# First attention: GpSimd masks the weights and ScalarE sums them, statistics are taken early; in roped attention the gathers, the first block and the PSUM banks are rearranged

## The chip, the cores and the metric

The kernel runs on one core of one Trainium2 chip, in one launch. Its time is the device time in microseconds, the median of several runs. PE is TensorE, DVE VectorE, ACT ScalarE, POOL GpSimd, SP the sync engine that issues most DMAs.

## The reference

Four layers, each of an attention and a feed-forward part, act on x (4 batches of 256 tokens, width 256) with a context of 1601 rows a batch; every part reads the layer-normed x and adds its result to x. The parts that matter here:

```
L0 attention:  Q = z @ Wq.T;  scores = coef * Q @ K_mem.T          # K_mem = V_mem = context, one head
               thr = 54th largest score of the row
               scores = where(scores < thr, -inf, scores)
               att = softmax(scores);  x += (att @ V_mem) @ W_o.T
L0 ffn:        top-2 of 8 experts; each token's two expert outputs, times its shares, are added to x
L1 attention:  16 query heads, 4 key heads of 128; q, k rms-normed, weighted, rotated (rope by position);
               keys = context + the 256 tokens (1857);  softmax(q @ k.T / sqrt(128)) @ v @ Wo.T
L3 attention:  the same without rope and with the context's keys alone (1601)
```

Everything is fp32. Products that need more than the PE's single pass are done as hi*hi + hi*lo + lo*hi, with hi and lo halves in fp32r.

## The kernel before

**First attention** (`memory_attention`). The 1024 queries are eight tiles j = 0..7 of 128, two a batch: b = j // 2, q = j % 2. Each engine runs its own queue, in an order written out in the code, and waits on semaphores.

PE per batch: `items(b)` (the context is turned to keys in eight pieces CX, the normed tokens NX, two projections Q; each is also split in hi and lo), `scores(b, q)`, `turn_weights(b, q)` (transposes the masked weights), `weighted(b, q)` (weights times context rows), `project(b, q)`. Its order is: turn_weights(b-1, 1), items(b+1) with weighted(b-1, 1) between its pieces, scores(b+1, 0), project(b-1, 1), turn_weights(b, 0), weighted(b, 0), scores(b+1, 1), project(b, 0). ACT keeps the raw scores (`keep`), takes exp, copies the turned weights (`take_weights`), and takes the high half of each item and output; a piece of an item goes back and forth between PE and ACT.

DVE finds the threshold. For each j it sorts the 1601 scores into four sets (`sort`, six two-input operations), then takes 28 steps of MAX8 and MATCH_REPLACE8 (`select`). Beside the sort and the first steps of j runs `merge(j - 1)`, eleven small operations of which the last gives the threshold of tile j-1. Right behind it, at step 5, came `mask(j - 1)`: one scalar_tensor_tensor (is_ge, then times exp) which also sums the row, and a reciprocal. At fixed steps DVE takes `output_low` and `add_output` of tile j-2: steps 2 and 7 in an even j, 14 and 20 in an odd one (OUTPUTS). At step 7 of an even j stood `row_stats(b + 1)`, at step 13 `normalise(b + 1)`. turn_weights of tile j waits for mask_ok; its second piece waits for y_done of tile j-1.

**Roped attention** (`grouped_attention` with rope). A first block (FIRST_TASKS) prepares batch 0 and head 0; then 16 groups (batch, key head) of 30 turns run, each group with two units of 15 key tiles (KT = 15). In turn n every engine does its part of score tile n, then the tasks of that turn in the list GROUP_TURNS; values(n) follow 21 turns later, the shift 18 turns later (on POOL for t % 4 == 0 and t >= 13, else on DVE), exp 20 turns later. Tasks work for the next group: KV (project one key tile), KN/KR (norm and rotate four key tiles; on POOL, in the first block on DVE), Q/QN/QR (queries; POOL), KX/QX (transposes), RA (nine steps on DVE that make angles of positions) and RS (their sines on ACT), W (split weights in hi and lo), OX/Y (output), MX/NB (row maxima), PX/PR (positions). `name<` is the task for the group before.

GP(j) on POOL gathers one of 16 expert outputs into a ring of four buffers (pairs j, two for each of 8 token tiles), GA(j) on DVE adds it to x; GP(j) waits for GA(j-4). Four pairs are in the first block, twelve in group 0.

PSUM: score tile n goes to bank SCORE_BANKS[n % 3] = (0, 1, 4); `scores(n)` on PE waits until `highest(n - 3)` on DVE has read its bank (`peaked`), or `keep(n - 3)` on ACT for the first tile of a unit. Items take ITEM_BANKS in turn, two in the groups: item i waits for `item_free` of item i-2. The second grouped attention (a3, no rope, KT = 13, 26 turns) has the same code and its own lists.

Of the kernel before, what the change touches and what calls it, by code (L numbers as in the profile page):

```python
# [151 lines left out]
def memory_attention(nc, m, w):  # L152
# [17 lines left out]
    with Stage(nc, "a0") as st:  # L170
        zt = [st.sb(f"zt{i}", [P, DC, S], F32R) for i in range(2)]
        ct = [st.sb(f"ct{i}", [P, DC, CTXP], F32R) for i in range(2)]
        stats, mv, rstd, z = (st.sb("stats", [P, QT, 6]), st.sb("mv", [P, QT, 2]), st.sb("rstd", [P, 2, QT]),
# [11 lines left out]
        best = st.sb("best", [P, 8])  # L185
# [10 lines left out]
            st.sem(n) for n in "item_ready item_hi item_rest item_free s_ready raw_ok neg_ok exp_ok mask_ok".split()]  # L196
        taken, padded, sort_ok, merged, minus_ok, pt_turned, pt_ok, o_ready, o_hi, o_lo, y_ready, y_done = [
# [50 lines left out]
        with nc.Block(name="a0_all") as block:  # L248
# [194 lines left out]
            def _(act):  # L443
# [67 lines left out]
                for b in range(B):  # L511
                    if b:
                        take_weights(b - 1, 1)
                        exp(b, 0)
# [9 lines left out]
                    take_weights(b, 0)  # L524
                    take_output(b, 0)
                    if b + 1 < B:
                        keep(b + 1, 1)
                take_weights(B - 1, 1)
                take_output(B - 1, 1)

            @block.gpsimd
            def _(pool):
# [4 lines left out]
                for b in range(B):  # L537
                    pool.wait_ge(var_ok, b + 1)
                    pool.tensor_tensor(rstd[:, 1, :], rstd[:, 0, :], m.nhalf[:, 0:1].to_broadcast([P, QT]),
                                       ALU.pow).then_inc(rstd_ok, 1)  # L540
# [3 lines left out]
            def _(dve):  # L544
                step = Step(dve, dstep)

                def row_stats(b):
                    for q in range(QT):
                        ins = dve.bn_stats(stats[:, q, :], m.x[:, QT * b + q, :])
                    step(ins)  # L550
                    for q in range(QT):
                        ins = dve.bn_aggr(mv[:, q, :], stats[:, q, :])
                    step(ins)
                    dve.tensor_scalar(rstd[:, 0, :], mv[:, :, 1], 1e-5, None, ALU.add).then_inc(var_ok, 1)

# [54 lines left out]
                def merge(j):  # L610
# [3249 lines left out]
```

## Time and profile before

| | us |
|---|---|
| median of 3 runs (lowest, highest) | 3559.38 (3558.9, 3567.83) |
| the profiled execution | 3562.59 |
| its span | 3560.9 |
| mean granted clock of PE in it | 0.959 |

| engine | busy us | share of the span |
|---|---|---|
| PE | 3303.9 | 93% |
| DVE | 2288.8 | 64% |
| ACT | 2254.4 | 63% |
| POOL | 1548.8 | 43% |

A busy share is an average over stages with different limits. A row of a timeline reads: start, duration of the merged instructions, engine, line, operation, out<-in, shapes, count; and in brackets the idle time of the engine before it and what ended it. Neighbouring instructions on DVE and ACT overlap by some 0.1 us at their ends, so the step from one start to the next is a little shorter than the duration.

### The profile page before, as it was taken

The page shows a single profiled execution, that of the slowest core. Times are in us where ns is not written, and L with a number is a line of the kernel's source. Part 1 is how long each engine was busy: PE and PEld are TensorE (multiplying, and loading weights), DVE is VectorE, ACT ScalarE, POOL GpSimd, SP SyncE. Part 2 cuts the span into 40 slices and gives each one's busy share as a digit, 9 for nine tenths or more (in the row PEclk, how much of TensorE's full clock was granted, in tenths as well). Part 3 has the DMA queues.
Part 4 walks back from the last instruction along what each step waited for, and adds up shares of the span by engine and source line. Part 5 has one row for each costly group of instructions (what it writes and reads, how often), then busy time and mean ns, then how long its engine had stood idle before and what let it go on. Part 6 is the DMA issues. An engine that isn't in the chain of part 4 may idle for free. (4 is left out here: it accounts for less than half of the span.)

```text
span 3560.9 us, 64151 instructions
## 1 busy us (share of the span) xinstructions
PE 3303.9 (93%) x23332; PEld 2863.1 (80%) x23332; DVE 2288.8 (64%) x4549; ACT 2254.4 (63%) x5204; POOL 1548.8 (43%) x1568
## 2 busy tenths in 40 slices
PE   6858968999999999998899999898999999999989
PEld 5658956889989989997666666587999999999888
DVE  8976756776676676666777777535655555555544
ACT  3426746777777777775476676516777777777743
POOL 0012136776676667673120220103555555555534
PEclk8879978999999999999899999899999999999999
DMA  5206522211120120001201000113221121110011
GB/s 191 93 25 230 213 101 69 87 61 37 43 79 31 37 91 31 31 19 50 86 1 38 10 29 1 77 38 119 77 77 60 42 73 42 64 64 31 31 39 39
DMA packets 74457, 227.83 MB, mean 64 GB/s; under 512 B 7780, under 2 KB 29472, under 8 KB 69152
## 3 DMA queue, kind: packets, MB, share of 16 engines
q1 hardware_dynamic: 67538, 184.04, 14.6%
q0 software_dynamic: 3696, 37.68, 2.8%
q8 instruction: 188, 3.08, 0.4%
q10 hardware_dynamic: 2910, 2.01, 0.2%
q14 instruction: 125, 1.02, 0.1%
HBM read 178.60 MB, written 45.11 MB: 63 GB/s over the span
## 5 line engine op out<-in xcount | busy, mean ns | idle before, releaser
L1188 PE MATMUL ps<-a_v_rows,a_ring 128*128 128x129 f32 (+1 forms) x7168 | 934.9, 275 | 15.2 <-DVE a_o_rows L1598 14.6
L1572 DVE SCALAR_TENSOR_TENSOR a_peak<-ps,a_k_rstd,a_peak 128x512 f32<-128x512 f32 (+1 forms) x768 | 575.8, 750 | 557.7 <-ACT a_ring L1309 546.5
L1309 ACT ACTIVATE a_ring<-ps,a_k_rstd 128x512 f32<-128x512 f32 (+1 forms) x896 | 618.2, 691 | 479.1 <-PE ps L1178 439.7
L1188 PEld LDWEIGHTS ps<-a_v_rows,a_ring 128*128 128x128 f32 (+1 forms) x7168 | 874.7, 191 | 35.5 <-issue 18.6
L1436 POOL TENSOR_TENSOR a_ring<-a_ring,a_negb 128x512 f32<-128x512 f32 (+1 forms) x506 | 645.6, 1297 | 266.0 <-ACT a_negb L1318 258.5
L1324 ACT ACTIVATE a_ring<-a_ring 128x512 f32<-128x512 f32 (+1 forms) x896 | 564.6, 633 | 12.3 <-DVE a_ring L1589 11.5
L1176 PE MATMUL ps<-a_qt,a_kt 128*128 128x512 f32 (+1 forms) x896 | 424.5, 474 | 9.4 <-DVE a_peak L1572 4.4
L1076 PEld LDWEIGHTS ps<-a_wr,a_ct 128*128 128x128 f32 (+1 forms) x2496 | 352.4, 189 | 57.4 <-issue 14.1
L1076 PE MATMUL ps<-a_wr,a_ct 128*128 128x256 f32 (+1 forms) x2496 | 374.0, 287 | 20.5 <-DMA a_ct<-ctx_lo 13.9
L1178 PE MATMUL ps<-a_qt,a_kt 128*128 128x512 f32 (+1 forms) x896 | 356.0, 397 | 0.0
L1177 PE MATMUL ps<-a_qt,a_kt 128*128 128x512 f32 (+1 forms) x896 | 354.6, 396 | 0.0
L3431 ACT ACTIVATE a_probs<-ps 128x1024 f32<-128x1024 f32 x224 | 229.9, 1026 | 135.4 <-PE ps L3285 134.7
L1589 DVE TENSOR_TENSOR a_ring<-a_ring,ps 128x512 f32<-128x512 f32 x390 | 263.0, 677 | 2.8 <-ACT a_negb L1318 2.8
L3623 DVE TENSOR_REDUCE a_parts<-ps 128x1 f32<-128x448 f32 x384 | 222.2, 619 | 57.3 <-PE ps L3247 52.2
L1178 PEld LDWEIGHTS ps<-a_qt,a_kt 128*128 128x128 f32 (+1 forms) x896 | 166.3, 186 | 42.7
L1176 PEld LDWEIGHTS ps<-a_qt,a_kt 128*128 128x128 f32 (+1 forms) x896 | 169.7, 189 | 13.0 <-issue 6.3
L1177 PEld LDWEIGHTS ps<-a_qt,a_kt 128*128 128x128 f32 (+1 forms) x896 | 169.7, 189 | 1.7
L3285 PE MATMUL ps<-a_qt,a_kt 128*128 128x512 f32 x448 | 164.3, 448 | 2.5 <-ACT a_qt L3418 2.3
L1371 POOL TENSOR_SCALAR a_k_sq<-a_k_sq 128x4 f32<-128x4 f32 (+2 forms) x128 | 29.9, 233 | 310.6 <-ACT a_v_rows L1272 306.1
L1520 DVE TENSOR_TENSOR a_k_rows<-ps,a_kw 128x128 f32<-128x128 f32 (+1 forms) x448 | 126.6, 283 | 54.0 <-ACT a_v_rows L1272 53.8
L3247 PE MATMUL ps<-a_kt,a_qt 128*128 128x448 f32 (+1 forms) x512 | 154.7, 369 | 4.6 <-ACT a_kt L3399 1.1
L1268 ACT ACTIVATE a_square<-ps 128x128 f32<-128x128 f32 (+1 forms) x448 | 125.0, 279 | 36.9 <-PE ps L1076 30.6
(469 smaller groups left out, 6028.8 us busy)
## 6 DMA issues: line engine op xcount, KB each, us to landing
a_wr<-a_w SPq DMA_DIRECT2D x96, 512.0 KB, 4.4
a_w<-a_wr SPq DMA_DIRECT2D x32, 512.0 KB, 3.9
a_wr<-a_w SPq DMA_DIRECT2D x48, 256.0 KB, 3.6
a_ct<-ctx_hi SPq DMA_DIRECT2D x8, 1090.0 KB, 6.1
a_ct<-ctx_lo SPq DMA_DIRECT2D x8, 1090.0 KB, 8.8
f_we<-in_f_experts SPq DMA_DIRECT2D x8, 1088.0 KB, 8.3
ctx_hi<-a_ct SPq DMA_DIRECT2D x4, 1602.0 KB, 5.4
ctx_lo<-a_ct SPq DMA_DIRECT2D x4, 1602.0 KB, 9.3
```

What stands on the lines that cost most here:

```text
L1076: ins = pe.matmul(out[0:r, 0:2 * HD], src, wr[0][v][:, c * 2 * HD:(c + 1) * 2 * HD], start=(n == 0), stop=(n == 3 * DC - 1))
L1176: pe.matmul(out, kt[0][:, at:at + r], qt[0][:, cols], start=True, stop=False)
L1177: pe.matmul(out, kt[0][:, at:at + r], qt[1][:, cols], start=False, stop=False)
L1178: pe.matmul(out, kt[1][:, at:at + r], qt[0][:, cols], start=False, stop=True).then_inc(st_ready, 1)
L1188: ins = pe.matmul(m.ps[:, 6 + i // 2, (i % 2) * 256:(i % 2) * 256 + VW], slot(n)[0:r, i * P:(i + 1) * P], v_rows[u // NG % 2][0:r, t, :], ...
L1309: act.activation(slot(n)[0:r, :], m.ps[0:r, SCORE_BANKS[n % 3], :], ACT.Copy, scale=k_rstd[0:r, g % 2, t:t + 1]).then_inc(kept, 1)
L1324: act.activation(slot(n)[0:r, :], slot(n)[0:r, :], ACT.Exp).then_inc(exp_done, 1)
L1436: pool.tensor_tensor(slot(n)[0:r, :], slot(n)[0:r, :], negb[0:r, u % 2, :], ALU.add)\
L1572: dve.scalar_tensor_tensor(out=peak[0:r, :], in0=m.ps[0:r, SCORE_BANKS[n % 3], :], scalar=k_rstd[0:r, u // NG % 2, t:t + 1], in1=(slot(n - ...
L1589: dve.tensor_tensor(slot(n)[0:r, :], slot(n)[0:r, :], m.ps[0:r, MAX_BANK, :], ALU.add)\
L3431: act.activation(flat2(probs[n % 3][:, :, :]), flat2(m.ps[:, first:first + 2, :]), ACT.Exp)\
L3623: dve.tensor_reduce(to, slot(("R", h, j))[:, 0:n], AX.X, ALU.max, negate=True).then_inc(neg_done, 1)
```

## The change

In first attention, `mask` goes to POOL as two passes (is_ge against the threshold into a new tile `above`, then times exp in place), ACT sums the masked row in a copy with an accumulator (`sum_weights`, behind each `take_weights`), and DVE takes the reciprocal at `add_output`. The threshold is handed on by a nop on DVE behind a wait for the last MAX8, and `best` gets two buffers. The statistics of batches 1 to 3 are taken at once ahead of the first sort, in `powers(1)` on POOL too, and `normalise(b + 1)` moves from step 13 to step 7.

```
+                def sum_weights(b, q):                                  # ACT
+                    act.wait_ge(mask_ok, j + 1)
+                    act.activation(raw[b % 2][:, q, 0:CTX], expd[:, q, :], ACT.Copy, accum_out=rsum[:, 0, q:q + 1])\
+                       .then_inc(sum_ok, 1)
...
                     if b:
                         take_weights(b - 1, 1)
+                        sum_weights(b - 1, 1)
                         exp(b, 0)
                     if b + 1 < B:
                         items(b + 1)
...
                     take_weights(b, 0)
+                    sum_weights(b, 0)
                     take_output(b, 0)
...
                 take_weights(B - 1, 1)
+                sum_weights(B - 1, 1)
                 take_output(B - 1, 1)
...
+                def mask(b, q):                                         # POOL
+                    j = QT * b + q
+                    pool.wait_ge(chosen, j + 1)
+                    pool.tensor_scalar(above[:, :], raw[b % 2][:, q, 0:CTX], best[j % 2][:, AT:AT + 1], None, ALU.is_ge)\
+                        .then_inc(above_ok, 1)
+                    pool.wait_ge(above_ok, j + 1)
+                    pool.wait_ge(exp_ok, j + 1)
+                    pool.tensor_tensor(expd[:, q, :], expd[:, q, :], above[:, :], ALU.mult).then_inc(mask_ok, 1)
...
-                        dve.max(out=best[:, :], in_=rest).then_inc(merged, 1)
+                        if r == 0 and j >= 2:
+                            dve.wait_ge(above_ok, j - 1)
+                        ins = dve.max(out=best[j % 2][:, :], in_=rest).then_inc(merged, 1)
+                        if r == LEFT_ROUNDS - 1:
+                            dve.wait_ge(merged, base + 2 * LEFT_ROUNDS - 1)
+                            dve.engine_nop().then_inc(chosen, 1)
...
                 def add_output(b, q):
+                    dve.wait_ge(sum_ok, QT * b + q + 1)
+                    step(dve.reciprocal(rsum[:, 1, q:q + 1], rsum[:, 0, q:q + 1]))
                     dve.wait_ge(y_ready, QT * b + q + 1)
...
                 dve.wait_ge(xs_in, 16)
+                row_stats(range(QT, TT))
...
-                        if j and i == FOLLOW:
-                            mask(*divmod(j - 1, QT))
...
                         if q == 0 and b + 1 < B and i == FOLLOW + 2:
-                            row_stats(b + 1)
-                        if q == 0 and b + 1 < B and i == FOLLOW + 8:
                             normalise(b + 1)
```

In roped attention the two lists of turns change, and in both grouped attentions the banks:

```
 GROUP_TURNS True:
-        "Y0< KR6< PR0 GP4 GP5", "MX1 KR7< GP6 GP7", "NB1 KX2< W0< PX0", "Q0 RA0 GA4 GA5 GP8 GP9", "Y1< RS0",
-        "Q1 GA6 GA7 GP10 GP11", "KX3<", "QN0 W2< RA1 RA2 GA8 GA9 GP12 GP13", "KV0 QN1", "KV1 QR0 GA10 GA11 GP14 GP15",
-        "KV2 QR1", "KV3 QR2 RA3 GA12 GA13", "OX0 KN0 QR3 GA14 GA15", "KV4 KR0", "KV5 KR1", "KV6 W1 RA4", "MX0", "NB0 QX0",
-        "KV7 RA5", "KX0 KN1", "KV8 KR2", "KV9 KR3", "KV10 RA6", "OX1 N0", "KV11", "KX1 KN2", "KV12 KR4 RA7",
-        "KV13 KR5 NZ0", "KV14 RA8", "QX1 KN3 NX0",
+        "Y0< KR6< PR0 GP4 GP5 GP6 GP7", "MX1 KR7<", "NB1 KX2< W0< PX0", "Q0 RA0 GA12< GA13<", "Y1< RS0 GA14< GA15<", "KX3<",
+        "Q1", "W2<", "KV0 QN0 GA4 GA5", "KV1 QN1 GA6 GA7", "KV2 QR0", "KV3 QR1 RA1 RA2", "OX0 KN0 QR2", "KV4 QR3", "KV5 KR0",
+        "KV6 W1 KR1 RA3 GP8", "MX0 GP9", "NB0 QX0 GP10", "KV7 RA4 GP11", "KX0 KN1", "KV8 KR2", "KV9 KR3", "KV10 RA5 RA6 GA8",
+        "OX1 N0 GA9", "KV11 GA10", "KX1 KN2 GA11", "KV12 KR4 RA7 GP12", "KV13 KR5 NZ0 GP13", "KV14 RA8 GP14",
+        "QX1 KN3 NX0 GP15",
 FIRST_TASKS True:
-        "GP0 V0 GP1 GP2 GP3 PR0 PX0 GA0 GA1 RA0 RA1 GA2 GA3 RA2 N0 RA3 KV0 NZ0 KV1 RA4 NX0 KV2 V1 KV3 RA5 Q0 KV4 RA6 "
-        "Q1 KV5 QN0 RA7 KV6 QN1 RA8 KV7 RS0 KN0 KR0 KV8 KR1 KN1 KX0 KV9 QR0 KR2 KV10 QR1 KR3 KV11 KX1 QR2 KN2 QR3 W1 "
-        "KV12 KR4 QX0 KV13 KR5 KV14 KX2 KN3 QX1 KR6 W0 KR7 KX3"
+        "GP0 V0 GP1 GP2 GP3 PR0 PX0 RA0 RA1 RA2 GA0 GA1 GA2 GA3 N0 RA3 KV0 RA4 NZ0 KV1 V1 RA5 NX0 KV2 RA6 KV3 RA7 Q0 KV4 Q1 "
+        "RA8 RS0 QN0 KV5 KR0 KN0 QN1 KV6 KR1 KX0 KV7 QR0 KN1 KR2 KV8 QR1 KR3 KV9 KX1 KV10 QR2 KV11 KN2 QR3 KR4 KV12 KR5 "
+        "QX0 W1 KV13 KX2 KV14 KN3 KR6 QX1 KR7 W0 KX3"
...
-    SCORE_BANKS, MAX_BANK = (0, 1, 4), 5
+    SCORE_BANKS, MAX_BANK = (0, 1), 5
-            ITEM_BANKS = (2, 3) if attend else (2, 3, 6, 7)
+            ITEM_BANKS = (2, 3, 4) if attend else (2, 3, 6, 7)
...
-                        if n >= 3:
-                            if (n - 3) % KT:
-                                pe.wait_ge(peaked, peaks(n - 3))
-                            else:
-                                pe.wait_ge(kept, n - 2)
+                        if n >= 2:
+                            if (n - 2) % KT:
+                                pe.wait_ge(peaked, peaks(n - 2))
+                            else:
+                                pe.wait_ge(kept, n - 1)
```

The other uses of the score bank (in `scores`, `keep` and `highest`) go from `n % 3` to `n % 2`.

## Rows read from the trace of the kernel before

**Rows 1.** The windows by stage: busy us of each engine, granted clock, DMA share, GB/s.
```profile
0.00:240.00 240.00, 171.37 (x961) 145.86 (x961) 210.96 (x604) 81.20 (x142) 5.46 (x18) 0.82 0.29 106
...
480.00:540.00 60.00, 27.81 (x130) 24.70 (x130) 35.16 (x66) 19.97 (x75) 25.53 (x31) 0.61 0.33 119
...
540.00:605.00 65.00, 53.41 (x289) 44.35 (x290) 43.19 (x70) 40.25 (x109) 47.44 (x49) 0.84 0.24 78
...
605.00:1665.00 1060.00, 1040.42 (x7550) 955.90 (x7549) 720.17 (x1248) 781.90 (x1937) 705.20 (x713) 1.00 0.14 49
```

**Rows 2.** DVE's timeline in first attention: start us, us, instruction, idle before.
```profile
25.46 1.90 DVE L585 TENSOR_TENSOR a_sorting<-a_raw 128x802 f32<-128x802 f32 x2 [4.49 <-ACT a_raw L474]
...
34.53 0.73 DVE L549 BATCH_NORM_STATS2 a_stats<-x_slots 128x6 f32<-128x256 f32 x2
...
167.09 0.47 DVE L643 SCALAR_TENSOR_TENSOR x_slots<-ps,a_rsum,x_slots 128x256 f32<-128x256 f32 x1
...
180.84 0.28 DVE L618 MAX8 a_best<-a_found 128x8 f32<-128x120 f32 x1
...
181.50 1.88 DVE L629 SCALAR_TENSOR_TENSOR a_expd<-a_raw,a_best,a_expd 128x1601 f32<-128x1601 f32 x1
```

**Rows 3.** PE's timeline in first attention.
```profile
39.59 1.08 PE L301 MATMUL ps<-ident,a_z 128*128 128x128 f32 x4 [3.60 <-DVE a_z L561]
...
133.78 0.65 PE L373 MATMUL ps<-ident,a_expd 128*128 128x128 f32 x4 [0.74 <-DVE a_rsum L632]
...
164.31 0.94 PE L413 MATMUL ps<-a_wr,a_ot 128*128 128x256 f32 x6 [0.27 <-DVE a_ot L636]
...
183.82 0.60 PE L373 MATMUL ps<-ident,a_expd 128*128 128x128 f32 x4
...
227.21 1.97 PE L373 MATMUL ps<-ident,a_expd 128*128 128x128 f32 x8 [5.81 <-DVE a_rsum L632]
```

**Rows 4.** POOL's groups by form: busy us, mean ns, idle before.
```profile
L3478 POOL TENSOR_TENSOR a_k_rows<-a_k_rows,a_norm_w 128x1024 f32<-128x1024 f32 x6 | 14.3, 2391 | 0.5
...
L3477 POOL TENSOR_TENSOR a_k_rows<-a_k_rows,a_sq 128x1024 f32<-128x1024 f32 x6 | 11.4, 1898 | 0.5
...
L1798 POOL CAST f_wr<-f_wf 128x1024 fp32r<-128x1024 f32 x14 | 14.5, 1038 | 92.0 <-PE ps L1905 92.0
```

**Rows 5.** Line L1436 by itself: duration ns min/median/max, first and last start.
```profile
L1436 POOL TENSOR_TENSOR a_ring<-a_ring,a_negb x506: 1257/1285/2317, 579.4 to 3418.1; 128x512 f32<-128x512 f32 x128, 65x512 f32<-65x512 f32 x41
```

**Rows 6.** ACT's timeline in first attention.
```profile
137.06 1.62 ACT L481 ACTIVATE a_expd<-a_raw,a_negm 128x1601 f32<-128x1601 f32 x1
```

**Rows 7.** ACT's, DVE's and PE's timelines in roped attention's first block.
```profile
510.02 1.28 ACT L1331 ACT_TABLE_LOAD   x1
...
510.69 0.65 DVE L1645 TENSOR_SCALAR a_ang_tmp<-a_ang_tmp 128x960 f32<-128x960 f32 x1
...
515.73 1.08 PE L1105 MATMUL ps<-ident,a_k_rows 128*128 128x128 f32 x4 [5.52 <-DVEq L1534]
...
537.70 0.77 PE L1105 MATMUL ps<-ident,a_k_rows 65*128 65x65 f32 x3 [3.92 <-DVEq L1534]
```

**Rows 8.** DVE's, PE's and POOL's timelines in group 0 of roped attention.
```profile
561.48 3.79 DVE L1498 SCALAR_TENSOR_TENSOR x_slots<-a_z,share,x_slots 128x256 f32<-128x256 f32 x2 [2.28 <-DMA a_z<-y_slots,slot]
...
565.99 0.80 PE L1176 MATMUL ps<-a_qt,a_kt 128*128 128x512 f32 x1 [4.39 <-DVE a_peak L1572]
...
578.52 0.73 POOL L1399 TENSOR_TENSOR a_k_rows<-a_by_cos,a_by_sin 128x256 f32<-128x256 f32 x1
```

**Rows 9.** PE's waits in roped attention: us in total, times, longest.
```profile
PE ps L1133 <- DVE a_qt L1489: 3.5, 3, 1.2
```

**Rows 10.** PE's timeline in a steady group of roped attention.
```profile
836.36 2.02 PE L1188 MATMUL ps<-a_v_rows,a_ring 128*128 128x129 f32 x16 [0.30 <-DVE a_o_rows L1598]
```

**Rows 11.** PE's and DVE's timelines, second grouped attention, turns 20 and 18.
```profile
2475.77 0.40 PE L1176 MATMUL ps<-a_qt,a_kt 128*128 128x512 f32 x1
...
2476.95 0.75 DVE L1572 SCALAR_TENSOR_TENSOR a_peak<-ps,a_k_rstd,a_peak 128x512 f32<-128x512 f32 x1 [2.17 <-ACT a_ring L1309]
```

More of the change, by code:

```diff
@@ L184, in memory_attention @@
         found = [st.sb(f"found{i}", [P, FOUND, 8]) for i in range(2)]
-        best = st.sb("best", [P, 8])
+        best = [st.sb(f"best{i}", [P, 8]) for i in range(2)]
+        above = st.sb("above", [P, CTX])
         expd = st.sb("expd", [P, QT, CTX])
@@ L196, in memory_attention @@
             st.sem(n) for n in "item_ready item_hi item_rest item_free s_ready raw_ok neg_ok exp_ok mask_ok".split()]
+        chosen, above_ok, sum_ok = [st.sem(n) for n in "chosen above_ok sum_ok".split()]
         taken, padded, sort_ok, merged, minus_ok, pt_turned, pt_ok, o_ready, o_hi, o_lo, y_ready, y_done = [
@@ L536, in _, with powers @@
                     pool.memset(ct[i][:, :, CTX:CTXP].bitcast(F32), 0.0).then_inc(zeroed, 1)
[L537 to L540, printed above, removed]
+                def powers(part, cols):
+                    pool.wait_ge(var_ok, part + 1)
+                    pool.tensor_tensor(rstd[:, 1, cols], rstd[:, 0, cols],
+                                       m.nhalf[:, 0:1].to_broadcast([P, cols.stop - cols.start]), ALU.pow).then_inc(rstd_ok, 1)
+                def mask(b, q):
+                    j = QT * b + q
+                    pool.wait_ge(chosen, j + 1)
[4 more added lines that the diff above has]
+                    pool.tensor_tensor(expd[:, q, :], expd[:, q, :], above[:, :], ALU.mult).then_inc(mask_ok, 1)
+                powers(0, slice(0, QT))
+                powers(1, slice(QT, TT))
+                for j in range(QT * B):
+                    mask(*divmod(j, QT))
                 token_powers(pool, m, "f0", EARLY)
@@ L621, in merge @@
                             dve.wait_ge(merged, base + 2 * r + 1)
-                            dve.match_replace(out=rest, in_to_replace=best[:, :], in_values=rest, imm_value=-3.0e38)\
+                            dve.match_replace(out=rest, in_to_replace=best[j % 2][:, :], in_values=rest, imm_value=-3.0e38)\
                                .then_inc(merged, 1)
                             yield
-                    dve.wait_ge(merged, base + 2 * LEFT_ROUNDS - 1)
-                def mask(b, q):
-                    dve.wait_ge(exp_ok, QT * b + q + 1)
-                    step(dve.scalar_tensor_tensor(out=expd[:, q, :], in0=raw[b % 2][:, q, 0:CTX],
-                                                  scalar=best[:, AT:AT + 1], in1=expd[:, q, :],
-                                                  op0=ALU.is_ge, op1=ALU.mult, accum_out=rsum[:, 0, q:q + 1]))
-                    dve.reciprocal(rsum[:, 1, q:q + 1], rsum[:, 0, q:q + 1]).then_inc(mask_ok, 1)
                 def output_low(b, q):
@@ L658, in _ @@
                 dve.wait_ge(x_in, 16)
-                row_stats(0)
+                row_stats(range(QT))
                 dve.wait_ge(kact, 2)
@@ L702, in _ @@
                 add_output(B - 1, 0)
-                mask(B - 1, 1)
                 dve.wait_ge(y_done, QT * (B - 1))
```

26 lines of the change are left out of this document (14 added, 12 removed).

## The prediction, made before the change was run

> **What bounds the kernel now.** I read the page first: PE is busy 93% of the span, so the question in each stage is what still makes PE wait. The windows give the stages [rows 1]: first attention 0 to 240 us (PE 171 of 240, DVE 211), roped attention's first block 480 to 540 (PE 28 of 60, granted clock 0.61), its group 0 from 540 to 605 (PE 53 of 65), its groups 1 to 15 (PE 1040 of 1060, clock 1.00). The two short stretches around 540 and the first attention have room; the long one has 20 us at most.
>
> In first attention j = 0..7 counts query tiles. DVE is gapless from 25.46 on in all but small pieces [rows 2], so it looks like the bound. But two of its steps wait for others. `add_output` of tile j-2 stands at step 20 of an odd j and needs PE's projection: for j = 5, PE ends it at 165.25 (164.31 + 0.94 [rows 3]), DVE takes it at 167.09 [rows 2], a slack of 1.84 us (1.44 for j = 3). And PE's `turn_weights` for tile 5 starts at 183.82 [rows 3] directly behind the mask (181.50 to 183.5 [rows 2]). So PE, ACT and DVE form a loop that is nearly closed: mask, turn, copies, exp, key items, scores, projection, `add_output`, end of j, merge, mask. That loop, and not the sum of DVE's work, is what I price.
>
> **First attention: the terms.** (1) The mask leaves DVE: 1.88 + 0.08, about 2.0 us a tile. (2) Statistics of b = 1 to 3, 0.73 + 0.25 + 0.17 from 34.53 on, about 1.13 us each, go into the 4.49 us in which DVE waited for the first raw scores [rows 2]: free. (3) `normalise` six steps earlier brings items(1) forward about 2.9 us (PE waited 3.60 us for z there, 39.59 [rows 3]). (4) A nop and a wait for the last MAX8, about 0.1 us; the threshold is handed on after that MAX8 (180.84 + 0.28 [rows 2]) and not at 181.50: 0.3 us earlier. (5) GpSimd's mask: no row shows it. The multiply is 1601 elements with two inputs; 1024 took 2.39 us [rows 4], hence 3.75 us (3.0 by the fastest two-input row, 1024 in 1.90 with a broadcast operand). The comparison has one input and a scalar: between the CAST row (1024 in 1.04, so 1.65 us) and the two-input row (3.75). I take 1.65, nearest in kind, and 0.2 for three handovers: 5.6 us, bounds 4.8 and 8. (6) ScalarE's sum: a 1601-element ACTIVATE takes 1.62 us [rows 6] and an accumulator read adds 0.1: 1.6 us a tile. For odd tiles it stands in ACT's queue ahead of exp(b+1, 0) and all key items of the next batch, for which PE waits (ACT is gapless there), so it counts in full. For even tiles PE's 8 us of weighted sums hide it, for tile 7 just so. (7) The reciprocal moves to `add_output`, ahead of its wait: hidden.
>
> Now the loop, tile 3's turn (133.78 [rows 3]) to tile 5's: before 50.0 us. After: + (5.6 - 2.0) for the mask, + 1.6 for the sum, - 1.84 of slack used up, - 0.3: +3.1 us. DVE has more than 5 us to spare at step 20, so its savings end in that wait. Step by step: tile 1's mask is ready at 84.2 (before 84.46: the earlier start just pays for GpSimd); tile 3's turn at 136.9 (+3.2); tile 5's at 189.5 (+5.7). In the last batch no items follow, DVE's saving counts again, tile 6's turn comes at 213.0 (+5.3), and since `output_low` of tile 6 holds the last merge, tile 7's at 235.8 against 227.21 [rows 3]: **+8.5 us** at the stage's end. The mask stands four times on this path: 4.8 us a mask gives +5, 8 us gives +18. What hides term (1) today is nothing; what makes it worthless is the wait at step 20.
>
> GpSimd's rate speaks against moving it. The Trainium skill (GPSIMD Engine Reference, section 3.1 Elementwise — side-by-side cycle accounting) puts a two-input operation at some 2.6 cycles an element and a one-input one near 1.03, at 1.2 GHz; an estimate from that page is 3.5 + 1.4 us, and the stage would then come out near +6. The rows above are slightly slower and stand.
>
> **First block of roped attention.** PE waits 5.52 us at 515.73 for the rotated keys, behind the sine tables (510.02 on ACT), behind the angles (510.69 + 0.65 on DVE) [rows 7]. The first three angle steps (2.5 us) now run in the gap before the gathered rows land, and the last one no longer stands behind two more projections' waits: I get angles at 508.1, tables at 510.0, first key transpose 2.8 us earlier. At the end the last rotation stands ahead of the weight split and not behind KX2, QX1 and W0: the last key transpose (537.70 [rows 7]) 2.4 us earlier. Rounded up for the smaller waits between: **-5.5 us** (bounds: 0, and -9 if half of PE's idle time goes).
>
> **Group 0.** GA8 to GA11 hold DVE for their gathers (2.28 us at 561.48 [rows 8]) and with it the scores: PE waits 4.39 at 565.99 [rows 8], and 3.50 and 1.09 in the 12 us after it. Twelve gathers, about 1.28 us each on POOL with issue, also stand among QN, QR and KR: keys 0 to 3 are rotated only at 579.25 (578.52 + 0.73 [rows 8]). In the new order only four stand ahead of them, before Q is there. POOL then has QN (4.3), four half rotations of q twice (8.2), KN0 (1.3), KR (4.0) from about 551 on: 569. PE's turn 19 needs it; four gathers (5.1) then delay the first shift to 574.4 and the turn of the first values from 585.7 to 576.6. **-9 us** (bounds -3, where POOL's later gathers delay the shifts, and -13, all of PE's waits and the slow clock).
>
> **Banks and steady groups.** The third item bank removes waits for item_free: 1.15 us three times (`Y`), 0.34 three times (`NX`), 1.48 once; the row of `Y`'s line sums 3.5 [rows 9]. `Q1` and `KX3` swapped: `outputs` now comes before Q1 on DVE, and the 0.30 us that PE waits for it in each of 12 groups (836.36 [rows 10]) goes; the three of 2.49 with the sine tables on ACT lose 0.2. Together 3.6 + 0.6 + 3.5 + 1.0 + 1.7 = 10.4. POOL's work shifted by a turn is hidden: QR3 is ready 7 us ahead of its reader. Against it, two score banks: scores(n) waits for peaked(n-2). I set each scores start against the end of the peak of two turns before: in groups past 0 the median margin is 1.2 to 3.5 us, so nothing is lost but about 0.3 us in the three groups with angle work. Roped groups: **-9.5 us** (bounds -2 and -11). In the second grouped attention the margins past group 0 are 0.64 us and up; in its group 0 they are negative: scores at 2475.77 started 1.93 us before that peak ended (2476.95 + 0.75 [rows 11]), turn 6 is short by 1.33. Less 0.8 for an item wait and recovery: **+2.5 us** (0 to +6).
>
> **Sum.** 8.5 - 5.5 - 9 - 9.5 + 2.5 = -13.0 us on the profiled execution's 3562.59 (3560.9 span and 1.7 around it). The median of the runs is 3.2 us below that execution, so I put it on the median: 3559.4 - 13.0 = 3546.4 us.
>
> **Rivals.**
> A. The group 0 and steady gains are small because POOL and the score banks take the waits' place: block -4, group 0 -3, steady -5, banks +3, first attention +8.5: 3559. For it: margins at turns 6, 7, 20 and 22 are the thinnest. Against it: POOL has idle time left in the second half of group 0 and half of the span [rows 1]. Chance 0.24.
> B. First attention gets faster: if ACT's sum and GpSimd's mask found slack that I don't see, DVE's 8 times 2 and 3.4 us would count, about -17 instead of +8.5: 3521. Against it: 1.84 us at step 20. Chance 0.09.
> C. Slower: GpSimd's mask is stretched by DVE, which is never idle in that stage. Rows show GpSimd's two-input operation from 1.26 to 2.32 us, median 1.29 [rows 5]. If both passes went at two-input rate and 1.75 times stretched, the mask would take 13.5 us, four times 7.9 more than I count: +40 in first attention, 3578. It decides from a mask of 11.5 us on (+32). Chance 0.09. The Trainium skill (SBUF — State Buffer, section Who interferes with whom) says that a DVE instruction with one SBUF input outside the two-port modes doesn't contend with GpSimd; MAX8 and MATCH_REPLACE8, which run behind the threshold, have one. No row here shows the pair.
> D. The change does what I say, within 8 us either way: 3546. Chance 0.58.
>
> **Chances.** D has 0.58, mostly beyond 0.3% (10.7 us, about what a measurement can tell from no change): 0.41 faster, 0.17 within. A is within: 0.22, 0.02 slower. B is faster, C slower. Faster 0.50, same 0.39, slower 0.11. The range 3533 to 3564 leaves out B, C and little else.
>
> **What would show it.** DVE waits for PE (y) at step 20 of j = 3 and 5, 5 us or more each; mask passes of 1.65 and 3.75 us on POOL; first attention ends near 249, not 240; group 0 starts 5.5 us sooner after its block's start and lasts 55; groups 4 to 6 take 69.25 and not 69.55; group 0 of the second one takes 44.5. If first attention ends before 238, or a steady roped group takes over 69.6, the prediction is wrong in its reasons.

## The result

The changed kernel takes 3568.27 us (median of 11 runs, 3565.64 to 3574.23), the kernel before 3563.39 us (11 runs, 3558.9 to 3567.83). The ratio is 1.0018, 95% interval 1.001 to 1.0027: slower by some 5 us. The forecast was 3546.4, with a range of 3533 to 3564: the result lies 22 us above the forecast and 4 above the range. Four of the 22 are no error of the forecast's terms: it stood on 3559.4, the median of the first three runs of the kernel before, and eleven runs give 3563.4. The profiled execution has a span of 3566.0 us, 5.1 more than before, where the forecast's terms summed to 13.0 less: 18 us apart.

The same stage boundaries in both profiled executions show where the forecast failed (the sum is taken before rounding). A boundary is the start of a PE instruction (the first transposes of the expert layer's z, the transpose of the positions, the first score tile of a group):

| stage | before, us | after, us | forecast | measured |
|---|---|---|---|---|
| first attention | 242.11 | 258.40 | +8.5 | +16.3 |
| first expert layer | 244.21 | 243.39 | 0 | -0.8 |
| roped attention, first block | 53.84 | 51.34 | -5.5 | -2.5 |
| its group 0 | 64.63 | 61.01 | -9 | -3.6 |
| its groups 1 to 14 | 987.74 | 978.61 | -9.5 | -9.1 |
| its last group, next layers | 854.14 | 855.34 | 0 | +1.2 |
| second grouped attention, group 0 | 42.04 | 45.89 | +2.5 | +3.9 |
| all behind it | 1072.2 | 1072.1 | 0 | -0.1 |
| sum | | | -13.0 | +5.2 |

### The profile page after: what moved, and what is told of

The parts are those of the page before. It is cut to its first block and busy times, and to the rows that moved or that the text cites. A ratio compares the mean times of both kernels' runs of the same rounds, so it can differ in the third digit from the quotient of the medians.

```text
span 3566.0 us, 64198 instructions
## 1 busy us (share of the span) xinstructions
PE 3298.7 (93%) x23332; PEld 2861.2 (80%) x23332; DVE 2279.9 (64%) x4531; ACT 2260.7 (63%) x5220; POOL 1606.0 (45%) x1582
## 5 line engine op out<-in xcount | busy, mean ns | idle before, releaser
L1393 POOL TENSOR_SCALAR a_k_sq<-a_k_sq 128x4 f32<-128x4 f32 (+2 forms) x128 | 28.8, 225 | 312.8 <-ACT a_v_rows L1294 308.3
```

## The profile after

The windows of the kernel after, for the stages of [rows 1] (columns as there: PE, PEld, DVE, ACT, POOL, granted clock, DMA share, GB/s):

```profile
0.00:258.40 258.40, 171.25 (x962) 145.51 (x962) 209.76 (x593) 93.54 (x158) 69.46 (x43) 0.81 0.27 98
501.80:553.00 51.20, 27.38 (x130) 25.04 (x130) 33.51 (x64) 19.48 (x74) 21.27 (x22) 0.63 0.31 114
553.00:614.00 61.00, 52.07 (x286) 43.71 (x287) 38.22 (x66) 39.64 (x108) 44.15 (x46) 0.90 0.24 79
614.00:1592.70 978.70, 970.25 (x7036) 894.43 (x7035) 671.04 (x1173) 732.08 (x1857) 676.77 (x693) 1.00 0.15 51
```

In first attention PE's busy time is that of before, 171 us, in a longer stage: the 16 us are waiting, not work. A stage's length in one execution isn't exact: over the profiles below, kernels with the same code in a stage differ by some 4 us in first attention, 3.7 in the first block (49.1 to 52.8 for the changed order, mean 50.6, with granted clocks of 0.63 to 0.74), and by 8.5 in the stage of the last group and the next layers (854.3 to 862.8). Group 0 of the second grouped attention repeats within 1 us, its other groups within 0.4.

POOL's two passes of the mask, by source line (ns min/median/max, first and last start):

```profile
L556 POOL TENSOR_SCALAR a_above<-a_raw,a_best x8: 4328/4330/4347, 55.6 to 236.4; 128x1601 f32<-128x1601 f32 x8
L560 POOL TENSOR_TENSOR a_expd<-a_expd,a_above x8: 3553/3564/3623, 60.0 to 240.8; 128x1601 f32<-128x1601 f32 x8
```

This is the row to read first. I had put the comparison at 1.65 us and the multiply at 3.75. The multiply came at 3.56, the comparison at 4.33, above the 3.75 of my two-input bound for it. The mask is ready 8.1 us behind the threshold: 5.6 were forecast, with 8 as the upper bound. All eight comparisons lie within 0.02 us, whatever DVE ran beside them, and the last multiply, at 240.83 when DVE was idle (from 240.78 to 253.99), took 3.55, the others 3.55 to 3.62: DVE doesn't stretch them.

PE's timeline at the turns of tiles 5, 6 and 7, against [rows 3]:

```profile
195.43 3.13 PE L375 MATMUL ps<-ident,a_expd 128*128 128x128 f32 x13 [7.91 <-POOL a_expd L560]
...
219.26 3.13 PE L375 MATMUL ps<-ident,a_expd 128*128 128x128 f32 x13 [10.08 <-POOL a_expd L560]
...
244.44 1.97 PE L375 MATMUL ps<-ident,a_expd 128*128 128x128 f32 x8 [11.39 <-POOL a_expd L560]
```

DVE's timeline at step 20 of j = 3 and 5 (`add_output` of tiles 1 and 3), against [rows 2], where DVE came to it without a wait:

```profile
118.52 0.48 DVE L669 SCALAR_TENSOR_TENSOR x_slots<-ps,a_rsum,x_slots 128x256 f32<-128x256 f32 x1 [4.50 <-PE ps L415]
...
173.19 0.48 DVE L669 SCALAR_TENSOR_TENSOR x_slots<-ps,a_rsum,x_slots 128x256 f32<-128x256 f32 x1 [3.86 <-PE ps L415]
```

So the loop is closed as forecast: what DVE saved by giving the mask away it spends here, and PE spends the mask's longer time at each turn.

PE's waits in roped attention's steady groups (after, 614 to 1665), against [rows 9]. The rows for `Y` and `NX` are gone, and two score banks cost 3.9. The wait for `outputs` fell to 5.3 from the 13.1 of the first row, which is the kernel before's (its groups 1 to 15, 605 to 1665):

```profile
PE ps L1188 <- DVE a_o_rows L1598: 13.1, 17, 2.5
PE ps L1210 <- DVE a_o_rows L1620: 5.3, 6, 1.1
PE ps L1198 <- DVE a_peak L1594: 3.9, 4, 1.1
```

## Experiments

The times stand beside the kernel before on the same chip in the same job (medians 3561.1 to 3562.3). Stages are read as in the table above. The changed first attention, in seven kernels that have it unedited, ended at 258.4 to 262.6, mean 260.7 (the profile after is the earliest of them); the one of before at 242.1 and 242.0 in two.

**The two halves.** Two kernels, each with a part of the diff undone: `memory_attention` (all that stands ahead of GROUP_TURNS) as changed and the rest as before; and the reverse.

> The kernel before with the whole edit of first attention and nothing of the roped one. My theory: the loop through add_output carries GpSimd's mask (8.1 us from the threshold on) four times, first attention's first expert transposes come at 258 us and not at 242, and nothing later gives it back: 15.5 us slower than the kernel before, 3579. Rival, the parts interact (the later entry into the expert stage changes PE's clock or a DMA): the two halves don't add up, this one is under 10 slower.

Measured: 3582.56 us, ratio 1.0051 (1.0037 to 1.0064): 18 us slower by the ratio, 21 by the medians. First attention ends at 262.61; no later stage differs from before by more than 3.8 us.

> The kernel before with the edit of the roped attention and of the banks alone, first attention as before. My theory: block -2.5, group 0 -3.6, steady groups -9.1, second attention's group 0 +3.9, rest 0: 11 us faster than before, 3552. Rival, interaction: more than 15 or less than 7 faster.

Measured: 3550.99 us, ratio 0.9967 (0.9955 to 0.9979), 12 us faster by the ratio, 11 by the medians, with block, group 0, steady groups and the second attention's group 0 at -3.0, -3.2, -9.1 and +4.0 (and +4.3 in the last group with the next layers, the stage that scatters most). The halves add up within the intervals: the change is a gain of 12 with a loss of 18 in front of it.

**The mask's price and its factor of four.** This kernel leaves the comparison out; the weights are multiplied by ones.

```
-                    pool.tensor_scalar(above[:, :], raw[b % 2][:, q, 0:CTX], best[j % 2][:, AT:AT + 1], None, ALU.is_ge)\
-                        .then_inc(above_ok, 1)
+                    if j == 0:
+                        pool.memset(above[:, :], 1.0).then_inc(above_ok, 1)
+                    else:
+                        pool.engine_nop().then_inc(above_ok, 1)
```

> The changed kernel with GpSimd's compare left out (the weights are multiplied by ones; the rest of first attention as it is): the mask is 3.6 and not 8.0 us behind the threshold. Loop theory: 4.35 us taken off a path that passes the mask four times, less what the waits at add_output (4.50 and 3.86 us) can give: 13 to 17 us faster than the changed kernel, expert transposes near 244. Rival 1, the loss comes from VectorE being held up while GpSimd's passes run (1.6 + 3.3 + 1.8 + 3.3 us seen at the two normalise pairs): only the part under the compare goes, about 5 us faster. Rival 2, ScalarE's sum carries the loss: under 3 us faster.

Measured: 3550.89 us, 17.4 below the changed kernel's 3568.27 (ratio to before 0.9967, 0.9955 to 0.9979; 16 us when each is set against the kernel before of its own job), and first attention ends at 241.27 and not at 258.40: 17.1 us for a pass of 4.33, so about four times (19.4 against the mean of the seven). By turns the gain is uneven: 1.7 us up to tile 1's turn, then 5.1, 3.5 and 7.8 up to those of tiles 3, 5 and 7. Rivals 1 and 2 are out. PE's timeline of this kernel at tile 3's turn (in the changed kernel it started at 140.75, after 7.90 us of waiting):

```profile
133.92 1.32 PE L375 MATMUL ps<-ident,a_expd 128*128 128x128 f32 x5 [3.55 <-POOL a_expd L562]
```

**Which of the comparison's properties makes it slow.** `best[j % 2][:, AT:AT + 1]` replaced by the number 0.0.

> The changed kernel with GpSimd's compare against the number 0 in the place of the tile's threshold (another set of weights is kept). The compare took 4.33 us, 2.7 ns an element, against my 1.65. Theory 1, that is what GpSimd takes for an is_ge on 1601 fp32 elements of a row: again 4.3 us, and the time of the changed kernel. Theory 2, the scalar held in SBUF, one for each partition, makes it slow: 1.6 to 3 us, and four times the difference comes off first attention (5 to 11 us).

Measured: 3569.1 us, ratio 1.002 (1.0011 to 1.0029). Its row by source line:

```profile
L556 POOL TENSOR_SCALAR a_above<-a_raw x8: 4257/4260/4282, 56.2 to 237.3; 128x1601 f32<-128x1601 f32 x8
```

Theory 1: GpSimd took 2.7 ns an element for this is_ge on fp32, more than for its two-input multiply (2.2). The operand from SBUF adds 0.07 us. Whether another operation in the same one-input form is faster, no run shows; the CAST of [rows 4] (1.0 ns) is another instruction.

**ScalarE's sum.** In ACT's order `sum_weights(b - 1, 1)` goes behind `items(b + 1)` (and `exp` waits for the sum of two tiles before).

> The changed kernel with ScalarE's sum of the odd tiles behind the next batch's key items instead of ahead of exp and those items. Loop theory: 1.6 us comes off the path at tiles 1, 3 and 5, the sum of tile 7 stays: 4 to 5 us faster than the changed kernel. Rival, the sum is hidden in GpSimd's mask time or delays the raw scores now: within 1 us.

Measured: 3567.4 us, ratio 1.0014 (1.0005 to 1.0023), 0.9 below the changed kernel; first attention ends at 256.90, 1.5 below the profile after and 3.8 below the mean of the seven. The forecast 4 to 5 us didn't come: the intervals of the two kernels overlap, and set against the kernel before of its own job this one is no faster than the changed one. So the sum costs less than the 1.6 us a tile that I counted in full. In the profile after PE waited only 0.90 us behind tile 3's sum, beside its own weighted sums:

```profile
148.03 0.50 PE L327 MATMUL ps<-a_ct,a_minus_r 128*128 128x512 f32 x1 [0.90 <-ACT a_ct L452]
```

How much of 0 to 4 us the three sums really cost, the runs don't tell.

**Normalise beside GpSimd's mask.**

```
-                        if q == 0 and b + 1 < B and i == FOLLOW + 2:
+                        if q == 0 and b + 1 < B and i == FOLLOW + 8:
```

> The changed kernel with normalise back at step 13, when GpSimd's mask of the tile before is over. In the changed kernel its two instructions took 1.99 + 3.72 and 2.50 + 3.72 us against 0.40 alone. Loop theory: VectorE gets some 5 us back twice, and they end in the wait at add_output (4.50 and 3.86 us): within 2 us of the changed kernel, the waits there grow. Rival, VectorE is held up by GpSimd and that is the loss: 5 to 10 us faster.

Measured: 3568.44 us, ratio 1.0018 (1.0009 to 1.0027): no change of the time, and DVE's waits at add_output grew from 4.50 and 3.86 to 5.7 and 5.0. In its profile first attention ended at 263.5, 0.9 above the longest of the seven, and not earlier. VectorE is held up, but off the path.

**Group 0: the gathers.** In the changed profile the first shift on POOL (590.10) stands behind three gathers. ACT's exp waits for it; behind that exp in ACT's queue stands the next `keep`, DVE's peak waits for that `keep`, and with two banks PE's score waits for that peak. POOL's, ACT's, DVE's and PE's timelines there:

```profile
586.50 1.08 POOL L1466 DMA_INDIRECT a_z<-y_slots,slot  x1 [0.31 <-POOL a_k_rows L1421]
587.89 0.95 POOL L1466 DMA_INDIRECT a_z<-y_slots,slot  x1 [0.30 <-issue]
589.14 0.95 POOL L1466 DMA_INDIRECT a_o_rows<-y_slots,slot  x1 [0.30 <-issue]
590.10 1.28 POOL L1458 TENSOR_TENSOR a_ring<-a_ring,a_negb 128x512 f32<-128x512 f32 x1
...
591.42 0.63 ACT L1346 ACTIVATE a_ring<-a_ring 128x512 f32<-128x512 f32 x1 [2.45 <-POOL a_ring L1458]
591.96 0.67 ACT L1331 ACTIVATE a_ring<-ps,a_k_rstd 128x512 f32<-128x512 f32 x1
...
592.66 0.75 DVE L1594 SCALAR_TENSOR_TENSOR a_peak<-ps,a_k_rstd,a_peak 128x512 f32<-128x512 f32 x1 [3.76 <-ACT a_ring L1331]
...
593.46 0.80 PE L1198 MATMUL ps<-a_qt,a_kt 128*128 128x512 f32 x1 [3.60 <-DVE a_peak L1594]
```

```
-        "KV6 W1 KR1 RA3 GP8", "MX0 GP9", "NB0 QX0 GP10", "KV7 RA4 GP11", "KX0 KN1", "KV8 KR2", "KV9 KR3", "KV10 RA5 RA6 GA8",
-        "OX1 N0 GA9", "KV11 GA10", "KX1 KN2 GA11", "KV12 KR4 RA7 GP12", "KV13 KR5 NZ0 GP13", "KV14 RA8 GP14",
-        "QX1 KN3 NX0 GP15",
+        "KV6 W1 KR1 RA3", "MX0", "NB0 QX0", "KV7 RA4 GP8", "KX0 KN1 GP9", "KV8 KR2 GP10", "KV9 KR3 GP11", "KV10 RA5 RA6",
+        "OX1 N0", "KV11 GA8", "KX1 KN2 GA9 GP12", "KV12 KR4 RA7 GA10 GP13", "KV13 KR5 NZ0 GA11 GP14", "KV14 RA8 GP15",
+        "QX1 KN3 NX0",
```

> The changed kernel with GP8 to GP11 of group 0 three turns later (turns 18 to 21, behind that turn's shift), and GA8 to GA11 and GP12 to GP15 after them. My theory: the first shift waited 2.45 us behind ScalarE's row and GpSimd's three gathers (586.5 to 590.1), and with it exp, keep(20), its bank and the scores (3.6 us): group 0 takes 57.5 and not 61.0, 3.5 us faster. Rival 1, the shift waits for KR1, which ends 33 us after the group's start: under 1 us. Rival 2, the gathers now stand among the later shifts and take it back: 0 or slower.

Measured: 3565.94 us, ratio 1.0014 (1.0005 to 1.0023), group 0 at 61.70. Turns 21 and 22 (from one score tile's start to the next) fell from 5.18 and 5.91 us to 2.74 and 3.22, and turns 25, 27 and 28 rose from 2.0, 2.3 and 2.3 to 3.34, 4.92 and 3.62: rival 2.

Only the fall of turn 21 is the wait of my theory. In turn 22 of the changed kernel PE never waits after its scores have begun; it runs at the lower clock (granted 0.51, near the 1.2 GHz level, against 1.00, 2.4 GHz, in this kernel's turn 22), behind a turn in which it was busy for 1.6 of 5.2 us. The windows of turns 21 and 22 of the changed kernel (columns as above):

```profile
588.28:593.46 5.18, 1.58 (x11) 1.24 (x9) 1.42 (x4) 2.73 (x8) 4.55 (x6) 0.90 0.32 89
593.46:599.38 5.92, 5.92 (x26) 5.63 (x26) 4.21 (x8) 3.37 (x11) 5.67 (x6) 0.51 0.03 11
```

Turn 28 of this kernel, with a clock of 0.62 behind the long turn 27, repeats it. Turn 27 shows something new. The addition GA9 on DVE took 3.63 us and not 0.48, until POOL's chain of three passes was through, and the peak and the scores stood behind it (this kernel's timelines of POOL, DVE, PE):

```profile
606.51 1.30 POOL L1458 TENSOR_TENSOR a_ring<-a_ring,a_negb 128x512 f32<-128x512 f32 x1
607.75 1.28 POOL L1413 TENSOR_TENSOR a_by_sin<-a_k_rows,a_cs 128x512 f32<-128x512 f32 x1
608.98 1.26 POOL L1414 TENSOR_TENSOR a_by_cos<-a_k_rows,a_cs 128x512 f32<-128x512 f32 x1
...
606.91 3.63 DVE L1520 SCALAR_TENSOR_TENSOR x_slots<-a_z,share,x_slots 128x256 f32<-128x256 f32 x1
610.46 0.74 DVE L1594 SCALAR_TENSOR_TENSOR a_peak<-ps,a_k_rstd,a_peak 128x512 f32<-128x512 f32 x1
...
611.26 0.50 PE L1198 MATMUL ps<-a_qt,a_kt 128*128 128x512 f32 x1 [2.38 <-DVE a_peak L1594]
```

The next kernel leaves gathers and additions of pairs 8 to 15 out (`return g == 0 and i < 8`).

> The changed kernel with only pairs 4 to 7 gathered and added in group 0; pairs 8 to 15 are left out (eight expert outputs are not added to x). Theory 1: the eight gathers and additions are what keeps group 0 from the forecast 55.6 us: group 0 takes 56. Theory 2: the chain of queries and keys on GpSimd, which ends 33 us after the group's start, keeps it: 59 or more.

Measured: group 0 takes 56.02 us (the whole 3560.18, ratio 0.9996, 0.9987 to 1.0005). Theory 1: the eight gathers with their additions are worth 5.0 us there, nearly the whole distance to the forecast 55.6. Two turns hold it: turn 21 fell by 2.4 us (the wait) and turn 22 by 2.7 (the clock, 1.00 here). The chain of queries and keys still ended 33 us after the group's start. The group behind it, whose first turns lose four additions too, took 67.0 and not 68.6.

**The first block.** In FIRST_TASKS:

```
-        "QX0 W1 KV13 KX2 KV14 KN3 KR6 QX1 KR7 W0 KX3"
+        "W1 KV13 KX2 KV14 KN3 QX0 KR6 QX1 KR7 W0 KX3"
```

> The changed kernel with the first block's end in another order: QX0 stands behind KV13, KX2, KV14 and KN3 and not ahead of them. My theory: the block's keys became early as forecast, and its end is now set by GpSimd's query chain, for which PE waited 4.06 us with two projections and a key transpose queued behind: the block takes 4 us less, 47 and not 51. Rival, the last keys' chain (projection, norm on GpSimd, rotation on VectorE, transpose) is as long: under 1 us.

Measured: 3562.31 us, ratio 1.0001 (0.9992 to 1.001), 6 us below the changed kernel. The block takes 46.77 us and not 51.34 (47.3 and 48.1 in the two later kernels with this order; the mean of eleven with the changed order is 50.6, so some 3 us are its worth). PE's timeline of the changed kernel and of this one; the wait of 4.06 for POOL's last half rotation is gone:

```profile
528.41 1.08 PE L1127 MATMUL ps<-ident,a_k_rows 128*128 128x128 f32 x4 [6.93 <-DVEq L1556]
...
542.98 1.09 PE L1136 MATMUL ps<-ident,a_q_rows 128*128 128x128 f32 x4 [4.06 <-POOLq L1422]
...
550.97 0.47 PE L1127 MATMUL ps<-ident,a_k_rows 65*128 65x65 f32 x3 [2.71 <-DVEq L1556]
```

```profile
541.41 0.63 PE L1127 MATMUL ps<-ident,a_k_rows 128*128 128x128 f32 x4 [2.09 <-DVEq L1556]
...
543.68 1.06 PE L1136 MATMUL ps<-ident,a_q_rows 128*128 128x128 f32 x8 [0.93 <-DVE a_kt L1511]
548.05 0.77 PE L1127 MATMUL ps<-ident,a_k_rows 65*128 65x65 f32 x3 [3.31 <-DVEq L1556]
```

Its group 0 took 58.05 us as well, 3 less, with the same list as in the changed kernel. The wait of turn 21 is there unchanged, but the clock did not fall behind it: turn 22 took 3.21 us at a granted clock of 1.00 and not 5.91 at 0.51. PE's timeline of this kernel, and the row of the same 16 matmuls in the changed one:

```profile
590.56 0.50 PE L1198 MATMUL ps<-a_qt,a_kt 128*128 128x512 f32 x1 [3.61 <-DVE a_peak L1594]
...
592.07 1.95 PE L1210 MATMUL ps<-a_v_rows,a_ring 128*128 128x129 f32 x16
```

```profile
596.19 3.43 PE L1210 MATMUL ps<-a_v_rows,a_ring 128*128 128x129 f32 x16
```

In the last kernel below, with the same lists, the clock fell (0.54 in turn 22) and group 0 took 60.50. A wait of 3.6 us there was followed by the lower clock in eight profiles of nine, a wait of 1.2 us in none of four; why this kernel was spared is not shown. So these 3 us can't be credited to its edit.

**The banks.** First two item banks for all grouped attentions, then, in another kernel, the banks of before for the second one alone:

```
-            ITEM_BANKS = (2, 3, 4) if attend else (2, 3, 6, 7)
+            ITEM_BANKS = (2, 3) if attend else (2, 3, 6, 7)
```
```
-    SCORE_BANKS, MAX_BANK = (0, 1), 5
+    SCORE_BANKS, MAX_BANK = ((0, 1) if rope else (0, 1, 4)), 5
-            ITEM_BANKS = (2, 3, 4) if attend else (2, 3, 6, 7)
+            ITEM_BANKS = ((2, 3, 4) if rope else (2, 3)) if attend else (2, 3, 6, 7)
```

> The changed kernel with two item banks in the grouped attentions again (two score banks kept, bank 4 unused). My theory: the waits for item_free come back, 1.15 us three times, 0.34 three times and 1.48 once: groups 1 to 14 of the roped attention take 6 us longer, 984.6 and not 978.6. Rival, what the steady groups gained comes from the order of Q1, KX3 and outputs alone: under 2 us.

Measured: 3571.66 us, ratio 1.003 (1.0019 to 1.0041), groups 1 to 14 at 982.75 and not 978.61: 4.1 us of the expected 6, and of the 9.1 that the steady groups gained. The waits are back where forecast (PE's waits, 622 to 1665); the 1.48 us one is not:

```profile
PE ps L1155 <- DVE a_qt L1511: 3.5, 3, 1.2
PE ps L1081 <- DVE a_k_rows L1542: 1.0, 3, 0.3
```

> The changed kernel with the old banks (three for scores, two for items) in the second grouped attention alone. My theory: its group 0 goes from 45.9 back to 42.0, its other groups stay at 62.0: 3.9 us faster than the changed kernel. Rival, the 3.9 us are the state of the clock at that place: no change of that group.

Measured: 3562.28 us, ratio 1.0 (0.9991 to 1.0009), the second attention's group 0 at 42.05, its others unchanged. PE's timeline of the changed kernel at [rows 11]'s turn, where now the score waits:

```profile
2480.98 0.50 PE L1198 MATMUL ps<-a_qt,a_kt 128*128 128x512 f32 x1 [1.81 <-DVE a_peak L1594]
```

**Versions that beat both.** The first takes the mask back to VectorE, with statistics and normalise early as in the change, and has e6's list and e7's banks. Its edit of the changed kernel's first attention, in short:

```
                        next(beside, None)
+                        if j and i == FOLLOW:
+                            mask(*divmod(j - 1, QT))
...
-                        sum_weights(b - 1, 1)
...
-                    sum_weights(b, 0)
...
-                for j in range(QT * B):
-                    mask(*divmod(j, QT))
```

> The kernel after with the mask on VectorE again (one pass with its sum, at step 5), but statistics and normalise early as in the change; the later gathers of e6; the old banks in the second grouped attention. First attention: VectorE keeps 3 times 1.13 us, as much as the slack of 1.4 and 1.8 us at add_output takes: 3 us faster than the kernel before, 239. With the rest: block -2.5, group 0 -7, steady -9.1, second group 0 0: 21 us faster than the kernel before, 3541. Rival, first attention doesn't gain and the gathers give nothing: 3549.

Measured: 3544.18 us, ratio 0.9947 (0.9933 to 0.9961); first attention ends at 237.64, group 0 takes 61.44.

The second adds e11's block and moves the later gathers across the group's border ("KV14 RA8 GA8 GA9", "QX1 KN3 NX0 GA10 GA11" at the end, "PR0 GP4 GP5 GP6 GP7 GP12< GP13<", "MX1 KR7< GP14< GP15<" at the start):

> The mask on VectorE with early statistics, the old banks in the second grouped attention, the block order of e11, and in group 0 GP8 to GP11 in turns 18 to 21, their four additions at turns 28 and 29 and GP12 to GP15 in group 1's first two turns. Against the kernel before: first attention -4, block -7, group 0 -6 (the additions no longer stand behind a chain of GpSimd passes ahead of a peak), steady -9: 26 us faster, 3536. Rival, group 1 takes back what group 0 gains (GpSimd's gathers stand ahead of KR6 and KR7): 3541.

Measured: 3538.92 us (3535.91 to 3541.35), ratio 0.9936 (0.9922 to 0.995); first attention ends at 236.05, block 48.13, group 0 57.68; group 1 took 71.68 against 68.58 after the change, the rival in part (one of its additions on DVE took 3.43 us and not 0.48). The third is the first with e11's block and the changed list of turns as it is:

> The mask on VectorE with early statistics and normalise, the block order of e11, the changed list of turns as it is, and the old banks in the second grouped attention. From the stages of the runs so far: 236.5 + 243 + 47 + 58 + 977.6 + 854.5 + 42.2 + 869.4 + 199.8, and 3 us ahead of and behind them: 3535 by the span, 3537 by the median. Rival, e12's order of the gathers was worth more than the 2.5 us that its group 1 gave back: over 3540.

Measured: 3539.13 us (3538.46 to 3541.19), ratio 0.9938 (0.9924 to 0.9951). Its block took 47.28, group 0 60.50, the steady groups 978.55. The last two are equal: some 23 us faster than before, 29 faster than the change.

## Why the prediction was wrong

**The step that failed is term (5), GpSimd's mask, mis-sized.** The comparison was priced by the CAST row [rows 4], "nearest in kind", at 1.65 us, with the two-input row (3.75) as the bound. It takes 4.33. The mask's 8.1 instead of 5.6 us, on the path four times, is +10. The prediction's own sentence "8 us gives +18" would have put the stage at 260; it measured 258.4, and 260.7 in the mean of seven. Had that stood in the sum, the forecast would have been 3556: a smaller gain than forecast, still no loss. Of the 18 us between the sum of terms and the profile, first attention has 8, group 0 has 5.4 and the first block 3. An operation that no row shows was taken at the low end of its bounds, and multiplied by four.

The figure near 1.03 cycles for a one-input operation, which the prediction quoted from the Trainium skill (GPSIMD Engine Reference, section 3.1 Elementwise — side-by-side cycle accounting), would have put the stage at +6; the measured 2.7 ns an element (3.2 cycles at that page's 1.2 GHz, an estimate) speaks against it for is_ge, and the measurement decides.

**What held in first attention.** The closed loop (waits of 4.50 and 3.86 at the two steps named, forecast 5 or more), the factor of about four (17.1 us for 4.33), the free early statistics (with them and the mask on VectorE first attention ends 4.5 to 6.5 us earlier than before in three kernels; I had expected 3). Term (6) was counted in full and cost less. The turns drifted as forecast and further: tile 3 at 140.75 (136.9 forecast), tile 5 at 195.43 (189.5), tile 7 at 244.44 (235.8). The forecast's own steps weren't even: it prices a turn at +3.1 us and then moves tile 5's turn by only 2.6 more than tile 3's.

**First block, -2.5 for -5.5.** The key side did what was said: the first key transpose comes 26.6 us after the block's start and not 29.4, 2.8 earlier. The last one was to win 2.4 more and lost 0.6 of the 2.8, since QX0 stands in PE's queue ahead of it and waits 4.06 us for POOL's queries (2.5 before); the step "the last key transpose 2.4 us earlier" left out who stands in the queue. Moved behind, the block gave 46.8 to 48.1 in three kernels, the forecast 48.3.

**Group 0, -3.6 for -9.** The lower bound (-3, "where POOL's later gathers delay the shifts") named the mechanism, and it is a part of what happened. From the group's start, the keys' rotation ended at 33.0 and not at 28.8 (POOL's chain began 2.5 us late and took 1.7 longer), the first shift came at 37.0 and not at 34.2, and turn 22, the turn of the first values, at 40.3 and not at 36.4. The step that failed is "four gathers (5.1) then delay the first shift to 574.4" with what follows it: it priced the gathers on POOL alone, and not exp and `keep` behind that shift in ACT's queue (2.4 us of turn 21), nor the clock, which fell behind that wait and made turn 22 2.7 us longer. Without the eight gathers and additions the group took 56.0 beside the forecast 55.6; that forecast had counted four of them in, so the closeness is in part luck.

**Steady groups, -9.1 for -9.5, and the second's group 0, +3.9 for +2.5.** The signs held, and groups 4 and 5 took 69.0 us as the prediction's own sign asked (69.25, not 69.55). That -9.1 lies so near -9.5 is luck: two terms missed by as much each way. Two score banks were to cost 0.3 us in the groups with angle work and cost 3.9 (1.1 in each of three such groups, 0.6 in group 1), and the waits for `outputs` were to give 4.2 and gave 7.8 (13.1 to 5.3 in the rows above), since the three of 2.49 fell to 0.93 and not to 2.3. The item bank's waits of 3.5 and 1.0 us returned when the bank was taken away; the sum of the terms also counted 1.7 where its text names 1.48 once. Group 1, which now has four of the additions, took 1.4 us longer than before. In the second, setting each score's start against the peak of two turns before gave the place: waits of 1.81, 1.21, 0.50 and 0.29 us stand against one item wait of 0.49 that went, 3.3 of the 3.9; the recovery in the deduction of 0.8 did not show.

**The rivals.** A's small terms came partly (block, group 0), without its first attention at +8.5. B fell at the waits that the profile shows. C's price was right in kind, a mask dearer than I counted (8.1, below its 11.5), but by the operation's rate and not by stretching.

## What to carry to other kernels

Before work is moved to GpSimd, price that very operation there: a comparison took longer than a two-input multiply of the same shape. A price that is paid at every turn of a closed loop multiplies its error. When one engine's list is reordered, read for each late item what stands behind it in every in-order queue that it passes; two of three misses here were a good move (the key chain, the gathers) with another waiting item left ahead of the one that was freed. A wait of TensorE can cost more than its length: behind 3.6 us the granted clock fell to 0.51, and the next turn took 2.7 us longer, so look at the granted clock of the stretch behind a wait before the loss is put down to waiting. And a bank or buffer traded between two users pays in one stage and costs in another: it should be set for each stage by itself.

## What the hardware showed that I had not expected

Some VectorE instructions wait for GpSimd's. `normalise` takes 0.40 us alone. Beside the mask, two of them as one row, in the changed kernel and in the one with normalise at step 13 (DVE's timelines):

```profile
79.90 5.63 DVE L588 TENSOR_SCALAR a_z<-x_slots,a_mv,a_rstd 128x256 f32<-128x256 f32 x2
...
134.70 6.14 DVE L588 TENSOR_SCALAR a_z<-x_slots,a_mv,a_rstd 128x256 f32<-128x256 f32 x2
```

```profile
141.82 3.39 DVE L588 TENSOR_SCALAR a_z<-x_slots,a_mv,a_rstd 128x256 f32<-128x256 f32 x2
```

The first instruction of the first pair ends 0.15 us after the comparison (77.41 + 4.33), the second 0.15 us after the multiply (81.83 + 3.55); in the third row the first one ends at 144.89, the multiply at 141.19 + 3.56 = 144.75. The mask's passes are not slowed; MAX8 and the scalar_tensor_tensor with an input in PSUM run on beside it. The Trainium skill (SBUF — State Buffer, section Who interferes with whom) says so: a two-input instruction with both in SBUF, or one in a two-port mode, waits for GpSimd's whole instruction when that came first. The trace agrees in the times (that `normalise`, with one input, runs in such a mode, no row shows), and adds that a chain of GpSimd instructions without a pause held VectorE for all three of them (3.63 us above).

GpSimd can be the one that waits. In group 0 of the changed kernel a rotation on GpSimd took 2.11 us and not the usual 1.28, begun 0.4 us behind a two-input instruction of VectorE and ending 1.1 us after it:

```profile
580.93 1.38 DVE L1498 TENSOR_TENSOR a_wr<-a_wf,a_wr 128x1024 fp32r<-128x1024 f32 x1 [0.66 <-ACT a_wr L1274]
...
581.33 2.11 POOL L1413 TENSOR_TENSOR a_by_sin<-a_k_rows,a_cs 128x512 f32<-128x512 f32 x1
```

The kernel before had the first kind too, and I misread it there: the addition of 3.20 us within the first row of [rows 8], which I put down to its gathers, lay beside these passes of POOL:

```profile
560.92 1.05 POOL L1384 TENSOR_TENSOR a_q_rows<-a_q_rows,a_q_sq 128x512 f32<-128x512 f32 x1
561.92 1.26 POOL L1391 TENSOR_TENSOR a_by_sin<-a_q_rows,a_cs 128x512 f32<-128x512 f32 x1
563.14 1.26 POOL L1392 TENSOR_TENSOR a_by_cos<-a_q_rows,a_cs 128x512 f32<-128x512 f32 x1
```

By the durations (3.20 against 0.48) 2.7 of PE's 4.39 us of waiting in that turn are this lock and not the DMA (an estimate: no run takes the chain away there). Moving the additions away from the gathers' landing doesn't remove it: in the changed kernel two of the first four still took 1.08 and 1.33 us. Moving them off POOL's chains might, but no kernel here does: in the second of the kernels that beat both, with the later additions at the end of group 0 and the start of group 1, two of them took 2.28 and 3.43 us.
